# AdaLN block with linear attention and a routed FFN: the set-up ahead of the block loop in a new order

## What is computed

```python
mod = (_silu(c) @ wmod).reshape(B, 6, 1, -1)       # sa, ca, ga, sb, cb, gb
ga = (2 * (ga >= 0) - 1) * maximum(abs(ga), 0.25)  # gb likewise
h = _layernorm(x) * (1 + ca) + sa
# attention: 16 heads of 16, 128 random features
q, k, v = split(h @ W_attn + b_attn); q, k scaled by 1/4
phi(t) = exp(t @ omega - 0.5 * sum(t * t)) / sqrt(128)
S = cumsum(phi_k * v); Z = cumsum(phi_k)
x = x + ga * ((phi_q @ S) / (phi_q @ Z + 1e-6) @ W_proj + b_proj)
h = _layernorm(x) * (1 + cb) + sb
# ffn: 4 experts, the best 2 of each token, rank 4 corrections B A
out = sum_e w_e * (relu(h @ Wi.T + lora_e(h)) @ Wo.T)
x = x + gb * out
```

## Time and profile before

| | |
|---|---|
| median of 3 runs | 803.96 us (803.41 to 805.09) |
| profiled execution, its own time | 803.24 us |
| its span | 801.0 us |
| busy in it: PE, DVE, ACT, POOL | 94%, 66%, 53%, 8% |
| chain that ended last: PE, DVE, issue, ACT, DMA | 80%, 11%, 3%, 2%, 2% |
| mean granted clock of PE | 0.986 |

### The profile page before, as it was taken

One profiled execution on the slowest core, in us unless ns is written; L12 is line 12 of the kernel. 1 busy time (PEld: TensorE's weight loads), 2 busy tenths in 40 slices (PEclk: granted clock), 3 DMA queues, 4 the chain that ended last, 5 costly groups with the idle time before them and its releaser, 6 DMA issues.

```text
span 801.0 us, 16997 instructions
## 1 busy us (share of the span) xinstructions
PE 751.1 (94%) x6138; PEld 607.2 (76%) x6138; DVE 531.3 (66%) x1264; ACT 427.0 (53%) x776; POOL 62.7 (8%) x72
## 2 busy tenths in 40 slices
PE   3889999999999999999999999999999999998696
PEld 3678768887698767887688867987688876986466
DVE  4366776676766776776776766767766766666356
ACT  3376636664557544665466644666366645563232
POOL 1260100001000010001000010001100010000100
PEclk9999999999999999999999999999999999999699
DMA  8750273104701073102901055101731048000000
GB/s 280 211 123 2 71 195 58 52 0 138 183 0 52 26 211 84 52 0 89 216 16 52 26 146 149 33 20 52 203 65 52 0 125 196 1 27 28 0 1 27
DMA packets 42805, 65.36 MB, mean 82 GB/s; under 512 B 5001, under 2 KB 19105, under 8 KB 42657
## 3 DMA queue, kind: packets, MB, share of 16 engines
q1 hardware_dynamic: 42784, 65.09, 30.1%
HBM read 39.91 MB, written 25.17 MB: 81 GB/s over the span
## 4 chain that ended last, share of the span: by engine, by line
PE 80%; DVE 11%; issue 3%; ACT 2%; DMA 2%; POOL 1%; DVEq 0%; SPq 0%; POOLq 0%; ACTq 0%
PE pa L531 11%; PE prod L544 7%; PE ring L388 5%; PE ring L510 5%; PE pa L388 5%; PE pa L390 5%; PE pa L389 5%; PE ring L389 4%; PE ring L390 4%; PE ring L564 4%; PE pa L646 4%; PE ring L515 3%; PE ring L674 2%; PE ring L571 2%; DVE am_phk L1122 2%
## 5 line engine op out<-in xcount | busy, mean ns | idle before, releaser
L531 PE MATMUL pa<-phq,phkT 128*128 128x128 f32 x768 | 101.2, 275 | 0.0
L1122 DVE TENSOR_TENSOR am_phk<-pa,const 128x512 f32<-128x512 f32 x112 | 77.0, 689 | 35.6 <-PE pa L531 34.6
L531 PEld LDWEIGHTS pa<-phq,phkT 128*128 128x128 f32 x768 | 95.3, 191 | 2.1
L1290 DVE SCALAR_TENSOR_TENSOR am_phk<-ring,am_phk 128x512 f32<-128x512 f32 x64 | 44.2, 691 | 53.1 <-PE ring L727 53.1
L939 ACT ACTIVATE qk_r<-phq 128x512 fp32r<-128x512 f32 x64 | 40.5, 632 | 63.7 <-DVE phq L1299 63.7
L388 PE MATMUL pa<-wo_r,qk_r 128*128 128x256 f32 x256 | 72.1, 282 | 0.6 <-DVE qk_l L1295 0.6
L390 PE MATMUL pa<-wo_l,qk_r 128*128 128x256 f32 x256 | 72.1, 282 | 0.0
L389 PE MATMUL pa<-wo_r,qk_l 128*128 128x256 f32 x256 | 71.8, 281 | 0.0
L510 PE MATMUL ring<-xq,omega_x 100*128 100x512 f32 x196 | 70.3, 440 | 1.6 <-DVE lora_w L1115 1.6
L869 ACT ACTIVATE phq<-ring 128x512 f32<-128x512 f32 x82 | 49.3, 602 | 36.1 <-PE ring L510 35.0
L869 ACT ACTIVATE phkT<-ring 128x512 f32<-128x512 f32 x98 | 58.3, 595 | 12.9 <-PE ring L510 12.6
(11 more groups left out here) (205 smaller groups left out, 1627.7 us busy)
## 6 DMA issues: line engine op xcount, KB each, us to landing
xq<-qk_parts SPq DMA_DIRECT2D x48, 512.0 KB
qk_parts<-qk_r SPq DMA_DIRECT2D x32, 256.0 KB, 4.8
qk_parts<-qk_l SPq DMA_DIRECT2D x32, 256.0 KB, 5.2
tok<-in_L_attn_x SPq DMA_DIRECT2D x8, 512.0 KB, 3.6
xr<-in_L_attn_x SPq DMA_DIRECT2D x8, 512.0 KB, 3.4
out_x<-tg SPq DMA_DIRECT2D x16, 256.0 KB, 2.2
norm_parts<-norm_r SPq DMA_DIRECT2D x16, 128.0 KB, 2.6
norm_parts<-norm_l SPq DMA_DIRECT2D x16, 128.0 KB, 3.0
```

Of the source, the lines that this page charges most:

```text
L531: mm = pe.matmul(score_bank(q, a)[:, tt], phkT[:, q % 2, a, tt], query(q)[:, a, tt], start=True, stop=True)
L1122: dve.tensor_tensor(am[:, 2 * (q % 2) + a, :].rearrange("p (c t) -> p c t", c=NT), score_bank(q, a)[:].rearrange("p (c t) -> p c t", c=NT) ...
L1290: dve.scalar_tensor_tensor(r2[:, f % 2, :], z_bank[f % 4][:], 0.0, rho, ALU.max, ALU.mult).then_inc(r2_done.sem, 1)
```

## The change

The set-up is reordered; the loop gets one more wait and is otherwise the same.

- SP: x of block 0 goes first, in two halves with a semaphore each, then the condition, `wmod`, and only then the constants.
- PE: three products of zeros (`warm(3)`, float32, 128 x 512) ahead of `setup_mods(0)`, and one more ahead of qk. Gates, mods(1) and the four Wi transposes move ahead of qk piece 3, values and norms(0, 1) in between the lead features. The LoRA transposes come before Wo's.
- SP: for the lead features only pairs 0 and 1 are fetched (ten DMAs: six of 128 KB and four of 8 KB, signal `lead_moved`). The second half of q and k is sent after that, then the other two pairs are fetched (`rest_moved`, ten DMAs), then the second half (`moved[1]`). The loop's first pass waits for `rest_moved`.
- ACT: the exponential of the condition comes before `normalize_rest(0)`. ACT copies the high part of Wi, DVE that of Wo (before it was the other way round).
- Banks: lead features use three banks instead of four; gates, Wi, Wo and LoRA get others.

```diff
+            for b in range(2):
+                load(ld_x[b], (tok[:, 2 * b:2 * b + 2, :], x_rows[0, :, 2 * b:2 * b + 2, :]))
             load(ld_cond, *((cT[:, k, :], cond[:, k * P:(k + 1) * P].rearrange("b p -> p b")) for k in range(KT)))
-            load(ld_x, (tok[:], x_rows[0]))
-            load(ld_const, (const[:], consts))
...
             load(ld_mod[0], *((wmod_raw[0][k], w_rows(wmod, k, slice(0, 2 * C))) for k in range(KT)))
+            load(ld_const, (const[:], consts))
...
+                def fetch(half, kinds, pairs, signal):
+                    rows = slice(2 * half * VA, 2 * (half + 1) * VA)
+                    wait(sp, qk_out[half], 0, qk_out[half].per)
+                    for kind in kinds:
+                        for copy, part in enumerate((0, 0, 1)):
+                            src = parts_out[part, 2 * half:2 * half + 2].rearrange("k (i r) t -> r k i t", r=PAIR_ROWS)
+                            sp.dma_start(xq[copy * PAIR_ROWS:(copy + 1) * PAIR_ROWS, half, kind, pairs]
+                                         .bitcast(F32), src[:, kind, pairs]).then_inc(signal.sem, 16)
+                    wait(sp, norm_out[half], 0, norm_out[half].per)
...
+                send(0)
+                send(1)
+                send_norms(0)
+                fetch(0, range(2), slice(0, 2), lead_moved)
+                send(2)
+                send(3)
+                send_norms(1)
+                fetch(0, range(2), slice(2, HALF), rest_moved)
+                fetch_all(1)
...
+            def warm(count):
+
+                pe.wait_ge(set_const.sem, 1)
+                for _ in range(count):
+                    pe.matmul(pb[1], state[:, 0, 0, :], state[:, 0].rearrange("p g m -> p (g m)"), start=True, stop=True)
...
+            warm(3)
+            setup_mods(0)
             pe.wait_ge(ld_const.sem, 16)
-            setup_mods(0)
             transpose1(0)
+            warm(1)
             pe.wait_ge(wa_low.sem, KT)
             pe.wait_ge(set_mod.sem, 2)
             for k in range(KT):
                 for j in range(2):
                     qk(0, j, [k])
             qk(0, 2)
+            setup_gate(0)
             norms(0, 0)
+            setup_wi(0)
+            setup_wi(1)
+            setup_mods(1)
+            setup_gate(1)
             qk(0, 3)
+            setup_wi(2)
+            setup_wi(3)
+            pe.wait_ge(om_done.sem, 1)
+            wait(pe, norm_split, 0, 1)
+            features(0, 0, range(RUN), lead=True)
             pe.wait_ge(wa_low.sem, 2 * KT)
+            pe.wait_ge(gates_sb.sem, 1)
+            pe.wait_ge(set_mod.sem, 4)
             values(0)
+            features(0, 0, range(RUN, TILES), lead=True)
+            pe.wait_ge(gates_sb.sem, 2)
             norms(0, 1)
...
+            features(0, 1, range(RUN), lead=True)
             setup_low()
+            setup_lora(0)
+            features(0, 1, range(RUN, TILES), lead=True)
+            setup_lora(1)
+            for q in range(4):
+                setup_wo(q)
...
             split_norm(0, 0)
             split_qk(0, 2)
+            setup_wi(0)
+            setup_wi(1)
+            setup_mods(1)
             split_qk(0, 3)
+            setup_wi(2)
+            setup_wi(3)
             dve.wait_ge(ld_vb.sem, 16)
             values(0)
             split_norm(0, 1)
-            setup_mods(1)
-            setup_late()
+            setup_lora(0)
+            setup_lora(1)
+            for q in range(4):
+                setup_wo(q)
```

More of the change, by code:

```diff
@@ L454, in values, with setup_wi @@
                         mm.then_inc(v_ps.sem, 1)
-            def setup_wi(k):
+            def setup_wi(q):
                 pe.wait_ge(ld_wi.sem, 16 * 2)
[L458 to L478, removed]
+                wait(pe, qk_split, 0, q + 1)
+                k, half = q // 2, q % 2
+                for t in range(4):
+                    mm = pe.transpose(wi_bank[q][:, t * P:(t + 1) * P],
+                                      wi_raw[half][:, t * C + k * P:t * C + (k + 1) * P], ident)
+                mm.then_inc(late_pe.sem, 1)
             def setup_low():
                 pe.wait_ge(ld_low.sem, 16 * 4)
-                wait(pe, exp_done, 0, 2 * TILES)
+                pe.wait_ge(late_vec.sem, 3)
                 for k in range(KT):
@@ L485, in setup_low, with setup_lora, setup_wo @@
                 mm.then_inc(late_pe.sem, 1)
+            def setup_lora(half):
                 pe.wait_ge(set_pool.sem, 9)
[L487 to L492, removed]
+                if half == 0:
+                    pe.wait_ge(late_vec.sem, 4)
+                else:
+                    pe.wait_ge(late_act.sem, 5)
+                for t in range(LORA_TILES):
+                    mm = pe.transpose(lora_bank[half][0:LROWS, t * P:(t + 1) * P], (mk1, mk2)[half][:, t, :], ident)
+                mm.then_inc(late_pe.sem, 1)
+            def setup_wo(q):
+                pe.wait_ge(ld_wo.sem, 16 * KT)
+                pe.wait_ge(late_vec.sem, 5 + q)
+                for t in range(2):
+                    for k in range(KT):
+                        f = (2 * q + t) * P
+                        mm = pe.transpose(wo_bank[q % 2][:, (t * KT + k) * P:(t * KT + k + 1) * P],
+                                          wo_raw[k][:, f:f + P], ident)
+                mm.then_inc(late_pe.sem, 1)
             def features(n, p, tiles=range(TILES), lead=False):
@@ L497, in features @@
                     tile = p * TILES + k
-                    dst = lead_bank[tile % 4] if lead else proj_bank(tile)
-                    if tile == 0:
+                    dst = lead_bank[tile % 3] if lead else proj_bank(tile)
+                    if tile == 0 and lead:
+                        pe.wait_ge(lead_moved.sem, 16 * 10)
+                    if tile == 0 and not lead:
                         wait(pe, moved[0], n, moved[0].per)
@@ L502, in features @@
                         wait(pe, moved[1], n, moved[1].per)
-                    if lead and tile >= 4:
-                        wait(pe, exp_done, n, tile - 3)
+                    if lead and tile < 3:
+                        pe.wait_ge(late_vec.sem, 2)
+                    if lead and tile >= 3:
+                        wait(pe, exp_done, n, tile - 2)
                     if not lead and 2 <= tile < 2 * TILES:
@@ L857, in features @@
                     tile = q * TILES + k
-                    bank_of = lead_bank[tile % 4] if lead else proj_bank(tile)
+                    bank_of = lead_bank[tile % 3] if lead else proj_bank(tile)
                     wait(act, proj_ps, n, tile + 1)
@@ L945, in _ @@
             act.wait_ge(set_act.sem, 2)
-            for half in range(2):
-                front_qk(0, 2 * half)
-                front_qk(0, 2 * half + 1)
-                front_norm(0, half)
-            setup_gates()
-            features(0, 0, range(TILES), lead=True)
-            features(0, 1, range(TILES), lead=True)
-            setup_late()
+            for j in range(3):
+                front_qk(0, j)
+            front_norm(0, 0)
+            setup_gate(0)
+            setup_wi(0)
+            setup_wi(1)
+            setup_gate(1)
+            front_qk(0, 3)
+            setup_wi(2)
+            setup_wi(3)
+            features(0, 0, range(TILES), lead=True)
+            front_norm(0, 1)
+            features(0, 1, range(RUN), lead=True)
+            setup_low()
+            setup_lora(0)
+            features(0, 1, range(RUN, TILES), lead=True)
+            setup_lora(1)
             def after_attend(n, front_next):
@@ L1053, in ln1_stats @@
             def ln1_stats(n, tiles=range(NT), first=False):
-                if first:
-                    dve.wait_ge(ld_x.sem, 16)
-                else:
+                if not first:
                     wait(dve, x_loaded, n - 1, 16)
                 for t in tiles:
+                    if first and t % 2 == 0:
+                        dve.wait_ge(ld_x[t // 2].sem, 16)
                     dve.bn_stats(stats[:, t, :], tok[:, t, :]).then_inc(ln1_vec.sem, 1)
```

155 lines of the change are left out of this document (89 added, 66 removed).

## The result

The changed kernel takes 823.86 us (median of 6 runs, 821.93 to 828.04) against 803.68 for the kernel before in the same session (6 runs, 803.04 to 805.09). The ratio is 1.0261, with a 95% interval of 1.023 to 1.0292: 20 us slower, where 2 to 3 us faster were forecast. The profiled execution took 823.8 us around a span of 821.6.

A forecast was written before the change was run, and what follows sets the result against it. The prediction took the loop as PE-bound and unchanged, so any gain had to come in the set-up: S 8.1 us sooner, a longer way to L, L 2.0 us sooner. 803.24 - 2.0 gave 801.3 us, range 799.3 to 804.0.

The forecast's parts named there:

- L: Start of the loop's first feature matmuls on PE: 53.89 before, forecast at 51.9, 2.0 us sooner.
- if the loop's own length changes: Sign of being wrong: from L to the end was to stay 747.1 us as before.
- qk at 15.5: Set-up on PE: qk's first matmul at 15.5 instead of 17.99, after h and one zero product.
- The clock in qk: Set-up on PE: clock rises some 1.5 us into qk, so qk 0 to 2 end at 20.8 instead of 24.88.
- The fetch from 26.1: Set-up on SP: norms sent by 26.1, then the fetch of two pairs of q and k for the lead features.
- S: Start of the lead features in the set-up: 40.47 before, forecast 32.4 (31.0 to 34.5), 8.1 us sooner.
- The fetch itself: Lead fetch of two pairs: six issues 2.8 us, four norm issues 1.0, landing 2.4; in at 32.3.
- Rival (5): Lead fetch set by number of DMAs, not bytes: 11.8 us, S 37.9, time 806.7 us; chance 0.05.
- S to L: Lead features to the loop's first features: 13.4 us before, longer because work now lies behind the DMA wait.
- The clock lost between the Wo blocks: PE's sparse stretch before L loses the high clock: 4.4 us at half speed, costing 2.2 us.
- Rival (2): The clock stays high through the Wo blocks: L 50.15, time 799.5 us; chance 0.15.
- rival (4): The front gains less, S = 34.4: 803.2 us, no difference; chance 0.15.

The follow-up runs named there:

- experiments 1, 4 and 5: Kernel before plus 27 PE instructions (met waits), 824.72 us; changed kernel without its four zero products, 803.77 us; four kernels with 12 to 23 more PE instructions, 804.81 to 835.42 us.
- experiment 5: Four single runs: changed kernel with one or three zero products, 805.98 and 824.59 us; kernel before with 12 or 19 more PE instructions, 804.81 and 835.42 us.
- Experiment 8: Changed kernel without zero products, omega's loads ahead of Wi's and Wo's, norms ahead of gate(0) on PE: 801.94 us, ratio 0.9973 against the kernel before.

## Why the prediction was wrong

**The step that failed** is the one on which the whole working rested: "The loop is bound by PE and the diff leaves its order alone, so whatever the change is worth must show before the loop's first own matmul", and from it "The loop itself should keep its times" and "from L to the end 747.1 us as before". From L to the end it took 821.6 - 56.37 = 765.2 us. That is one of the signs that the prediction named for being wrong ("if the loop's own length changes"), but it gave it no chance and no price. The order was left alone, but the instructions' places were not. I counted the zero products as time on an idle engine and costed them at nothing; they and the waits are also 27 instructions ahead of a loop, and experiments 1, 4 and 5 show that this alone is 20 us, by way of a jump that takes 3.3 to 3.6 us instead of 0.2. The 16 of the zeros were enough to cross the border, and 11 were not. None of my rivals had it, so the time lies 19.9 us above the range. The page of before had a row that I did not read: 13 packets on q8, so few that the loop cannot be read anew in every turn. It asks whether it still fits after the edit.

The Trainium skill (Runtime: NRT & Kernel Launch, Instruction fetch mechanics) says that PE's instruction memory holds 2048 instructions and is refilled in blocks of 256 (16 KiB), and that a taken branch to a target outside its window waits for a DMA. The traces agree in the packets of 16 KB and in the wait at the jump (1.9 to 3.6 us). The same section calls the window two pages; in the kernel before a body of 1624 instructions, over six blocks, ran six turns with no packet between 126.3 and 698.5 us, so for PE the measurement decides against that. Counted in the trace from the first instruction of the kernel's own PE program, the body of the kernel before stands behind some 355 instructions and ends near 1980. By the block size of that section of the Trainium skill I estimate that it begins in the second and ends in the eighth, and touches seven. The border that experiment 5 found, between 15 and 19 more, is then an end of 1995 to 2000, some 50 instructions short of 2048. If as many instructions stand ahead of the kernel's own, which is a guess, the body touches eight blocks with 19 to 27 more, and with 117 or 120 more it begins in the third and touches seven again, as the runs have it. Why eight blocks would not stay in a memory of eight stays open.

**The set-up, term by term.** This part missed by 4.5 us at L, 56.37 against 51.9.

- qk at 15.5: it was 14.02, 1.5 better. wmod was there at 7.24 and not at 8.3, mods took 2.66 us from then, and the zero product ahead of qk lay in time in which PE waited anyway.
- The clock in qk: I let it rise 1.5 us in. It was low from 8.3 to 18.5, so it rose 4.5 us into qk. The bounds beside it were mis-sized too: at the spacings of the earlier trace rows the 18 products take 4.2 us at the high clock and 7.7 at the low one, so from 15.5 they end at 19.7 or 23.2, where I had 18.5 and 22.4, and at 20.4 with 1.5 us of low clock, where I had 20.8.
- norm_l at 24.95: 24.56. The omega load, which I left at 21.3, landed at 21.32.
- The fetch from 26.1: it was 28.92. This is the mis-sized term of S. I had SP's issue of the norms as the last wait. But omega held DVE's splits, so all four sends of q and k were issued between 22.90 and 24.71, and the last landed only at 28.90, 4.64 us after its issue. My working had the 2.4 us of a norm send and did not ask when the sends of q and k land. Experiment 8 shows it: with omega sooner (and the norms ahead of gate(0)) the fetch begins at 24.64. PE's own way to S, which I put at 32.0, held: the last wi transpose begins at 31.93 there, and S is 32.31.
- The fetch itself, 6.2 us forecast: 28.92 to 35.14, 6.2 measured. Six issues took 2.69 us and four 1.17 (2.8 and 1.0 forecast). Rival (5), a fetch set by the number of DMAs, is out.
- S to L, 19.5 forecast: 21.0. The clock fell at 32.2, when the wait of 3.25 us for the fetch had just begun, behind a pause of 1.87 us and four transposes, and it stayed low until 39.0. The values behind the wait took 0.21 us each at first in place of 0.12, the exponentials of tiles 3 to 5 ended at S+7.25 and not S+5.4, and the second lora split at S+14.2, not S+12.25. From there the four pairs of Wo took 1.34 us each as forecast.
- The clock lost between the Wo blocks, 2.2 us forecast: it was 0.50 from 49.2 to 56.1, and the scores took 3.22 us where 1.95 was before. From the second pair of Wo to L it took 4.0 us, 4.55 forecast. Rival (2) is out. The Trainium skill (TensorE: Matmul & The Clock Gate, HAM oscillation) has the danger in long single gaps; here no gap after S was longer than 1.74 us, and the clock fell nevertheless, as in the earlier trace rows.

With the loop at its old length the changed kernel would have been at 801.3 + 4.5 = 805.8 by this count. The same set-up with one zero product was at 805.98 us, for 806.49 of the kernel before beside it, and with none at 803.77 for 804.19. So without the instruction memory it would have been no difference, near rival (4).

## What to carry to other kernels

A hardware loop has a place in instruction memory, and every instruction ahead of it moves that place: compare the packets of the instruction queue before and after any edit of a set-up, also one whose time is hidden. When every turn of a loop gets longer by the same few microseconds, and the engine waits at the loop's first instruction for nobody ("issue"), look there first. When work is moved out of a wait for a transfer to behind it, count it in full, and at the clock that the wait leaves behind.

## What the runs showed of the hardware

- PE kept a loop of 1624 instructions with no instruction packet for six turns. With 15 more instructions ahead of it that stayed so; with 19 to 27 more every turn read nine packets of 16 KB; with 117 and 120 more it read none.
- A turn that reads its instructions anew cost 2.2 to 4.3 us here, and 3.5 to 6.4 us just past the border. Nearly all of it is the wait at the jump, which took 3.3 to 3.8 us (4.7 to 5.0 just past the border) for 0.2, and the low clock that follows in some turns. Elsewhere in a turn PE's waits are those of before to a tenth in the kernel after.
- A wait that is already met is not free on PE: instructions with two such waits each began 0.11 us apart. 27 of them in idle time cost nothing; 120 moved mods(0) by 7.9 us.
- The three zero products of the kernel after did not hold the clock. It fell at 8.3, 2.1 us after they had ended at 6.23, and stayed low until 18.5, with the fourth product from 11.50 to 13.42 in between. With the fourth alone (experiment 5) the clock rose at 14.5, right at the start of qk at 14.40. Even so DVE had to wait for omega until 21.06, and L was 55.79, no more than L varies by itself from the 56.09 without any.
